# A graph layer on one core: PE's pipeline goes from three chunks to five, and the index loads get another release

## The reference

```python
h = jnp.maximum(_layernorm(x, axis=-1), 0.0)
e_feat = jnp.concatenate([h[src], h[dst], edge_attr], axis=-1)   # 412500 x 96
v = jax.nn.relu(e_feat @ W1 + b1) @ W2 + b2                      # 96 -> 64 -> 32
x_cand = jax.ops.segment_max(v, dst, num_segments=12500)
out = x + jnp.maximum(x_cand, h)
```

## Time and profile before

| what | value |
|---|---|
| median of three runs | 5345.29 us (5330.25 to 5361.33) |
| the profiled execution | 5326.15 us |
| its span | 5324.3 us |
| PE busy | 3680.6 us, 69% |
| PE weight load busy | 2578.9 us, 48% |
| GpSimd busy | 2701.2 us, 51% |
| VectorE busy | 2212.2 us, 42% |
| ScalarE busy | 982.3 us, 18% |
| mean granted TensorE clock | 0.829 |

### The profile page before, as it was taken

The page is one execution under the profiler, slowest core; times in us unless marked ns, Lnnn a source line. Parts: engine busy times, 40 slices in busy tenths (PEclk is TensorE's granted clock), DMA queues, the critical chain, the costliest instruction groups (busy, mean ns, idle before and its releaser), DMA issues.

```text
span 5324.3 us, 74917 instructions
## 1 busy us (share of the span) xinstructions
PE 3680.6 (69%) x19060; PEld 2578.9 (48%) x19060; DVE 2212.2 (42%) x6394; ACT 982.3 (18%) x2055; POOL 2701.2 (51%) x2853
## 2 busy tenths in 40 slices
PE   1577676667766777767776667676766767667777
PEld 1355454444544454545555445454544544445545
DVE  4344334344433444434444334343443443334436
ACT  2111111111111111111111111111111111111111
POOL 5455555554545455555555454555555555545551
PEclk9788888788888888888888888887887888878889
DMA  4222222222222222222222212222222222212222
GB/s 112 56 45 43 41 43 41 41 41 44 44 41 41 42 45 43 43 41 46 44 43 44 41 38 44 41 45 40 43 42 40 43 45 43 41 40 46 43 42 39
DMA packets 612176, 237.39 MB, mean 45 GB/s; under 512 B 328651, under 2 KB 609632, under 8 KB 612158
## 3 DMA queue, kind: packets, MB, share of 16 engines
q1 hardware_dynamic: 411534, 137.78, 10.7%
q0 software_dynamic: 91008, 46.57, 9.0%
q10 hardware_dynamic: 109616, 52.85, 3.4%
HBM read 227.75 MB, written 9.11 MB: 44 GB/s over the span
## 4 chain that ended last, share of the span: by engine, by line
another core or an unknown queue 43%; PE 29%; issue 14%; DVE 6%; ACT 5%; DVEq 1%; ACTq 1%; DMA 1%; SPq 0%
PE ps_spare L593 9%; PE ps_hid L547 5%; PE ps_hid L537 5%; PE ps_hid L543 3%; DVE hot L931 2%; PE ps_val L556 2%; PE ps_picked L578 2%; ACT hidden L726 2%; PE ps_turned L567 2%; PE ps_feat L528 2%; ACT feat_t L736 1%; ACT ps_biased L747 1%; DVE best L980 1%; ACTq L683 1%
## 5 line engine op out<-in xcount | busy, mean ns | idle before, releaser
L473 POOL DMA_INDIRECT feat<-h_rows,idx_ring x2824 | 2690.0, 953 | 2528.5 <-DMA idx_ring<-src_in 1661.4
L593 PE MATMUL ps_spare<-hot,table 128*128 128x256 f32 x10028 | 1920.8, 331 | 223.8 <-issue 221.0
L593 PEld LDWEIGHTS ps_spare<-hot,table 128*128 128x128 f32 x10028 | 1508.2, 212 | 574.4 <-issue 539.7
L980 DVE TENSOR_TENSOR best<-ps_picked,best 32x64 f32 x1612 | 354.8, 220 | 1495.6 <-remote 1358.8
L537 PE MATMUL ps_hid<-feat_t,w_blk 128*128 128x512 f32 x806 | 554.3, 777 | 515.9 <-ACT feat_t L736 387.0
L931 DVE TENSOR_SCALAR hot<-key_ring,class_at 128x256 fp32r<-128x256 f16 x2613 | 787.4, 369 | 98.3 <-remote 67.3
L726 ACT ACTIVATE hidden<-ps_hid,b_col 128x512 f32<-128x512 f32 x403 | 277.3, 688 | 1954.3 <-remote 1081.2
L567 PE MATMUL ps_turned<-ident,running 128*128 128x128 f32 x806 | 180.7, 310 | 567.9 <-DVE running L945 345.4
L547 PE MATMUL ps_hid<-edge_hot,term_ring 128*128 128x512 f32 x806 | 555.1, 776 | 0.7 <-DVE edge_hot L953 0.7
L967 DVE TENSOR_TENSOR ends<-ps_turned,ends 128x256 fp32r<-128x256 f32 x403 | 170.4, 423 | 731.7 <-ACT ends L731 416.3
L938 DVE SCALAR_TENSOR_TENSOR masked<-key_ring,group_at,ps_spare 128x256 f32<-128x256 f16 x400 | 174.0, 477 | 652.5 <-remote 584.3
(11 more groups left out here) (112 smaller groups left out, 1467.5 us busy)
## 6 DMA issues: line engine op xcount, KB each, us to landing
attr_ring<-edge_attr_in ACTq DMA_DIRECT2D x403, 128.0 KB
loc_ring<-loc_rows SPq DMA_DIRECT2D x403, 128.0 KB
feat<-h_rows,idx_ring POOLq DMA_INDIRECT x2824
keep_ring<-keep_rows SPq DMA_DIRECT2D x403, 64.0 KB
key_ring<-key_rows SPq DMA_DIRECT2D x201, 128.0 KB
term_ring<-term_rows SPq DMA_DIRECT2D x806, 16.0 KB
idx_ring<-src_in SPq DMA_DIRECT2D x403, 4.0 KB
end_ring<-end_rows SPq DMA_DIRECT2D x403, 2.0 KB
```

Of the source, the lines that this page charges most:

```text
L473: nc.gpsimd.indirect_dma_start(feat[:, slot, k, 0:D], None, h_dram, bass.IndirectOffsetOnAxis(ap=idx_ring[:, slot, k:k + 1].bitcast(U32), ...
L593: mm = pe.matmul(row_sums[t], table[half][:, at:at + Q, :].rearrange("p t d -> p (t d)"), hot[:, c, :], start=(c == 0 and t == 0 and half ...
L980: mm = nc.vector.tensor_tensor(col, ps_pick[D * q:D * q + D, WIN * q:WIN * q + WIN], col, ALU.max)
```

## The change

It does the following.

- PE's step now has features of v, first layer of v-1, second layer of v-2, turned ends of v-3 and picks of v-4. The selects of a batch lie in the last three gaps of an odd step and the first four of the next one. The steps of ScalarE and VectorE follow.
- PRE, the number of steps written out ahead of the loop, goes from 3 to 11; FULL = 3 takes over its other meaning, the chunks whose eight columns are all gathered.
- SyncE loads the index columns of chunk s when the gathers of chunk s-8 have landed. GpSimd then waits for `feat_turned` of chunk s-8 before it overwrites the slot. LAG goes from 2 to 4.
- `masked` gets two buffers by parity of the batch; the key rows are released by the mask of four batches before.
- The memset of `best` is split: the part that the start does not use is cleared early, the rest before the loop.

```diff
-PRE = 3
-LAG = 2
+FULL = 3
+PRE = 11
+LAG = 4
@@ SyncE
-            def step(s, slot, at):
-                sp.wait_ge(S["feat_turned"], s - (RING - 1))
+            def step(s, slot, turn, at):
+                sp.wait_ge(s_gather[slot], got(slot, turn - 1))
+                sp.sem_inc(S["idx_begun"], 1)
                 load_idx(at, slot)
                 if not known(s) or s - LAG >= RING:
                     sp.wait_ge(S["pick_ready"], s - (LAG + RING - 1))
                 load_aux(s - LAG, (slot - LAG) % RING)
@@
-                sp.wait_ge(S["mask_done"], i * 8 + 2 * (n - KEYS + 2))
+                sp.wait_ge(S["mask_done"], i * 8 + 2 * (n - KEYS + 1))
@@ GpSimd
                 pool.wait_ge(s_idx[slot], (i + v // RING) * 16 + 16)
+                if not known(i) or v >= RING:
+                    pool.wait_ge(S["feat_turned"], i * RING + (v - RING + 1))
@@ PE: first_layer
-                    pe.wait_ge(S["mask_done"], m * 2 + 4)
+                    pe.wait_ge(S["mask_done"], m * 2 + 2)
@@ PE: select
-                    if c == 0:
-                        pe.wait_ge(S["mask_done"], m * 2 + 2)
+                    if c == 0 and not (known(m) and m == 0):
+                        pe.wait_ge(S["mask_done"], m * 2)
@@ PE: order of a step
-            GAPS = (((0, 1), (2,), (3, 4), (5,), (6,)), ((7, 8), (9, 10), (11, 12), (), ()))
+            GAPS = (((6, 7), (8, 9), (10, 11), (12,), ()), ((), (), (0, 1), (2, 3), (4, 5)))
             def step(i, v):
...
+                m = i * 4 + (v - 1) // 2
+                gaps = GAPS[v % 2] if v else ((),) * 5
+                turn_features(i, v)
+                select(m, gaps[0])
+                if v >= 1:
+                    first_layer(i, v - 1)
                 select(m, gaps[1])
+                if v >= 2:
+                    second_layer(i, v - 2)
                 select(m, gaps[2])
+                if v >= 3:
+                    turn_ends(i, v - 3)
                 select(m, gaps[3])
+                if v >= 4:
+                    pick_ends(i, v - 4)
                 select(m, gaps[4])
@@ ScalarE
             def step(i, v, at):
+                take_features(i, v, at)
                 if later(i, v):
                     rectify(i, v - 1)
                 if later(i, v - 1):
+                    add_bias(i, v - 2)
+                if later(i, v - 2):
+                    take_ends(i, v - 3)
@@ VectorE
+            EARLY, LATE = range(0, 6), range(6, CLASSES)
             def step(i, v):
+                place_edges(i, v)
+                if v % 2 == 0:
+                    build_hot(i, v // 2, EARLY)
+                else:
+                    build_hot(i, v // 2, LATE)
+                if v >= 2:
                     scan(i, v - 2)
+                if v >= 2 and v % 2 == 0:
+                    mask_rows(i, v // 2 - 1)
+                if v >= 3:
+                    split_ends(i, v - 3)
+                    place_ends(i, v - 3)
+                if v >= 4:
+                    keep_best(i, v - 4)
```

More of the change, by code:

```diff
@@ L60, in gnn_layer @@
     assert ONE_TILE
-    assert D == 32 and HID == 64 and W2.shape[1] == D and (C - PRE) % RING == 0
+    assert D == 32 and HID == 64 and W2.shape[1] == D and (C - PRE) % RING == 0 and (C - FULL) % 2 == 0
     FULLP = N // T
@@ L152, in gnn_layer @@
         key_part = [z.bitcast(I32).rearrange("p (b e) -> p b e", b=NB)
-                    for z in (any_dst_h[:].rearrange("p b c -> p (b c)"), masked[:].rearrange("p t e -> p (t e)"))]
+                    for z in (any_dst_h[:].rearrange("p b c -> p (b c)"), masked[:, 0, :, :].rearrange("p t e -> p (t e)"))]
         key_stage = key_ring[:].rearrange("p k c a e -> p (k c a e)")[:, 0:NB * 2 * MIX].rearrange(
@@ L240, in got @@
             per = 16 * (COLS - 1)
-            return 16 * COLS + turn * per if slot < PRE else turn * per + per
+            return 16 * COLS + turn * per if slot < FULL else turn * per + per
         def any_steps(eng, any_step):
@@ L404, in _ @@
             for s in range(RING, ahead):
-                step(s, s % RING, s * CE)
+                step(s, s % RING, s // RING, s * CE)
             with sp.Fori(0, turns) as i:
@@ L412, in _ @@
             for s in range(ahead + RING * turns, C):
-                step(s, s % RING, s * CE if s < C - 1 else LAST)
+                step(s, s % RING, s // RING, s * CE if s < C - 1 else LAST)
                 if s % 2 == 0:
@@ L419, in _ @@
             next_key(0, BATCHES)
+            next_key(0, BATCHES + 1)
             sp.wait_ge(S["feat_turned"], C)
@@ L537, in first_layer @@
                 pe.matmul(ps_hid[:], w1_blk[:], feat_t[:, two, :], start=True, stop=False, skip_group_check=True)
-                if not known(i) or v >= PRE:
-                    m, part = i * 4 + (v - PRE) // 2, (v - PRE) % 2
-                    pe.wait_ge(S["mask_done"], m * 2 + 4)
+                if v >= FULL:
+                    m, part = i * 4 + (v - FULL) // 2, (v - FULL) % 2
+                    pe.wait_ge(S["mask_done"], m * 2 + 2)
                     for t in range(2):
-                        pe.matmul(ps_hid[HID:P, 2 * P:3 * P], w1_rep[:], masked[:, t, MIX * part:MIX * part + MIX],
+                        pe.matmul(ps_hid[HID:P, 2 * P:3 * P], w1_rep[:], masked[:, (v - FULL) // 2 % 2, t, MIX * part:MIX * part + MIX],
                                   start=False, stop=False, skip_group_check=True)
@@ L635, in clear_mixed @@
                 pe.wait_ge(S["cols_cleared"], RING)
-            steps(pe, step, {1: begin_mixed, PRE - 1: clear_mixed})
+            steps(pe, step, {0: begin_mixed, RING - 1: clear_mixed})
             first_layer(0, C - 1)
+            second_layer(0, C - 2)
+            turn_ends(0, C - 3)
+            pick_ends(0, C - 4)
+            second_layer(0, C - 1)
             turn_ends(0, C - 2)
-            second_layer(0, C - 1)
+            pick_ends(0, C - 3)
+            turn_ends(0, C - 1)
             pick_ends(0, C - 2)
-            turn_ends(0, C - 1)
             pick_ends(0, C - 1)
@@ L837, in _ @@
             nc.vector.memset(h_win[:, T - 1:Q * TG, :], 0.0).then_inc(S["pads"], 1)
-            for slot in range(PRE, RING):
+            for slot in range(FULL, RING):
                 nc.vector.memset(feat[:, slot, Q - 1, 0:D], 0.0).then_inc(S["cols_cleared"], 1)
@@ L905, in _ @@
             nc.vector.tensor_copy(key_stage[:, :, 1, :], high).then_inc(S["key_staged"], 1)
-            for t in range(2):
-                nc.vector.memset(masked[:, t, :], 0.0).then_inc(S["mask_done"], 1)
             dve.wait_ge(S["const_ready"], 5)
@@ L918, in _ @@
             nc.vector.engine_nop().then_inc(S["const_ready"], 1)
+            dve.wait_ge(S["loc_staged"], NB)
+            nc.vector.memset(best[:, T * HID:NP_ROWS], 0.0).then_inc(S["best_zero"], 1)
             node_terms(dve, nc.vector.tensor_copy, 1)
@@ L938, in mask_rows @@
                     nc.vector.scalar_tensor_tensor(
-                        out=masked[:, t, :].rearrange("p (c e) -> p c e", c=2), in0=key_ring[:, n % KEYS, :, 1, :],
+                        out=masked[:, n % 2, t, :].rearrange("p (c e) -> p c e", c=2), in0=key_ring[:, n % KEYS, :, 1, :],
                         scalar=group_at[:, t:t + 1], in1=row_sums[t].rearrange("p (c e) -> p c e", c=2),
@@ L1019, in _ @@
             dve.wait_ge(S["firsts_in"], 32)
-            steps(dve, step, {1: check})
+            dve.wait_ge(S["term_stored"], 16 * (1 + len(h_parts)))
+            nc.vector.memset(best[:, 0:T * HID], 0.0).then_inc(S["best_zero"], 1)
+            steps(dve, step, {0: check})
             scan(0, C - 2)
+            split_ends(0, C - 3)
+            place_ends(0, C - 3)
+            keep_best(0, C - 4)
+            scan(0, C - 1)
+            split_ends(0, C - 2)
+            place_ends(0, C - 2)
+            keep_best(0, C - 3)
+            split_ends(0, C - 1)
             place_ends(0, C - 1)
-            split_ends(0, C - 2)
             keep_best(0, C - 2)
-            scan(0, C - 1)
-            split_ends(0, C - 1)
             keep_best(0, C - 1)
```

67 lines of the change are left out of this document (14 added, 53 removed).

## The result

The changed kernel takes **5474.51 us** (median of four runs, 5470.36 to 5485.17). The kernel before, run beside it, takes 5337.77 (5261.16 to 5361.33). The ratio is 1.0341 with a 95% interval of 1.0223 to 1.0459: slower, where I forecast 4985 us and faster. The ratio counts fast runs only, for the kernel before the two of 5330.25 and 5261.16 us, which is why it is above the 1.0256 of the two medians. The profiled execution took 5477.52 us.

The account below looks back on a forecast made before the run. PE's semaphores, late while gathers fly, were taken to bound the loop. Lull 7.2, three chunks at 8.73 and landing 2.7 gave 11.9 us per chunk; 403 x 11.9 plus 189 gave 4985 us, range 4820 to 5260 (8 in 10: 4450 to 5520).

Parts of the forecast that it names:

- What bounds the kernel: The loop: while gathers are in flight PE works on, but its semaphores reach other engines late, over 4 us in one chunk.
- (a): PE's new step order: answers wanted a full step later, worth from nothing to 5.1 us per chunk.
- (c) and (d): Helper and key loads trailing further and two masked buffers, 0; split memset and deeper fill and drain, +10 us taken.
- short link: Class 0 of a batch waits for the previous batch's masking, an estimated 4.5 us; may stop PE once in two chunks.
- (b): Index load and GpSimd's wait: load released by landed gathers but queued behind helper loads; -2.60 to +4.6 us per chunk.
- lull: Time from PE's burst of signals until GpSimd starts gathering: 7.2 us after the change instead of 2.60.
- The sum: Cycle of lull 7.2, n chunks of gathers at 8.73 and landing 2.7 us, giving the period and 4985 us.
- n=3: Gathers in runs of three chunks (n is chunks per run), 11.9 us per chunk; n=2 would give 13.5.
- 19 us free: PE's unhindered time per three-chunk cycle: 7.7 step of tolerance, 7.2 lull, 4.5 of prompt signals, against 23 us needed.
- GpSimd starts later and its runs pair up: Rival at SyncE's queue: index load behind helper loads, runs of two chunks, 13.5 us per chunk, 5630 us; chance 0.30.
- Full gain: Rival: index load hidden nearly always, PE hardly ever stopped; 10.05 us per chunk, 4240 us; chance 0.16.
- The skill's trap: Rival: VectorE's fast modes lock GpSimd out of writing descriptors; gathers at an assumed 1.1 us, 5410 us; chance 0.03.

Follow-up runs that it names:

- late_gate: after_idx_ahead with GpSimd's chunk s also waiting until SyncE has issued the helper rows of s-5: 5284.68 us, 0.9874 of the kernel before.
- after_idx_ahead: The changed kernel with SyncE loading the index columns of s+2 in step s, ahead of its waits on PE: 4743.66 us, 0.8865 of the kernel before.
- grp_3_4: after_idx_ahead with each chunk's seven gathers in groups of three and four, GpSimd waiting between groups for their landing: 6131.4 us, 1.1506 of the kernel before.

## Why the prediction was wrong

**What bounds the kernel.** Right: the gathers make PE's signals late, and that is the loop (3151 us without them). One half of my sentence was wrong, "PE works on, but its semaphores reach the others late". In a long run PE itself stops, with no answer missing: "issue" ahead of single selects. From 2000 to 4000 us it is 84 us in the kernel before and 274 in the one after, at L593 and L598:

```profile
L593 PE MATMUL ps_spare<-hot,table 128*128 128x256 f32 x3900 | 753.5, 333 | 85.2 <-issue 84.0 <-DVE hot L931 0.9
...
L598 PE MATMUL ps_spare<-hot,table 128*128 128x256 f32 x3762 | 751.1, 342 | 439.5 <-issue 273.7 <-DVE masked L947 157.3 <-DVE best L989 7.7
```

Nor is it PE alone: SyncE's issues spread in a run too (2.9 us between two helper loads above). At the start 59 gathers run in a row, not the 56 that I counted, since three of the eight chunks gather eight columns; nothing hangs on it.

**(a) PE's order.** I gave nothing to 5.1 us a chunk. Measured, with (c) and (d) in it: 241 us with the old release (5351 to 5111 in its group), 94 with the load ahead, so 0.2 to 0.6 us. The short link that I named is there: the 157 us of waiting for `masked` above.

**(b) The index load.** The mechanism was right and the lull a little long. Between two runs I had 2.7 us of landing and burst and 7.2 of lull, 9.9 together; the trace has 9.1 on average, 8.05 to 9.82 in the four rows above. In the cycle shown, 3.2 us pass to the burst (3012.93 to 3016.12) and 5.3 from there to the first gather (3021.42). Its sign I left open, -2.60 to +4.6 us per chunk; it is a loss of 0.9 (5111 to 5475), and late_gate shows the lateness by itself, 541 us or 1.3 per chunk.

**(c) and (d).** Taken as neutral and +10 us. PE's wait at the start went from 17.25 to 12.77 us. No run did these parts alone, so their worth stays open.

**The sum: the step that failed.** "I take n=3, 11.9 us." The cycle has n=2, in 72 of 74 runs. The formula was nearly right: it gives 27.1 us for a cycle of two and the trace has 26.6 on average, 25.9 to 27.0 in the rows above; 403 chunks at 13.2 us are what the kernel takes. What failed is the reach of PE, "19 us free". I added PE's step of tolerance, the lull, and 4 to 5 us of prompt signals as if PE ran on at its own speed in a run. It went from one turn of features to the next in 18.4 us, three matmuls in some 7 us of it, so a third pick came in time in one of 74 runs. The row for it stood in front of me: picks recorded until 3072.26 with no answer before 3082.03, in a run of just two chunks. A tolerance of one step of 7.7 us can't span 10 us in which the engine that should use it is stopped as well.

**The rivals.** "GpSimd starts later and its runs pair up" is what happened, with the place and n as written. 13.5 us and 5630 were 2 to 3% too high (13.2 by the rows, 5475), since 9.1 us and not 9.9 lie between two runs. Its sign was there too, a period above 13 us with "remote" waits near 15 (12.8). I gave it 0.30 because PE's tolerance "is doubled or more", which counted steps and not time. "Full gain" does not come by this change, but after_idx_ahead shows how near it was: 11.3 us, still with late signals (7.66 us "remote" above, 1412 us in the whole run), not 10.05. "The skill's trap", from the Trainium skill, "SBUF — State Buffer", "Who interferes with whom": the trace agrees with it in kind, at a price far below the 1.1 us a gather that I assumed. From 2000 to 4000 us, 61 of the 219 gathers that run beside VectorE's `hot` or `edge_hot` take longer than 0.96 us, up to 1.19 (the one at 3008.17 above takes 1.01); of the 832 others none does, though many run beside other VectorE work. On average that is less than 10 ns a gather, and the mean stays at 949 to 958 ns in every kernel that gathers seven columns. By "TensorE: Matmul & The Clock Gate", "The cost: per-tile semaphore tail" (Trainium skill), a signal costs 26 ns; that may hold where nothing is gathered, but 12.8 us ahead of a copy is not in it.

## What to carry to other kernels

A load's release is not only the semaphore that its wait names but all that its queue has ahead of it: count the waits and issues between, and put the load whose landing starts a long stretch of work first, a chunk or two ahead. When a resource runs in bursts that silence another, a later start of the burst makes it longer, and the loss feeds itself; take the cycle's length from the time that the slower party really gets, not from how many steps it may run ahead. And test a reordering with each of its halves alone: here one half was worth 4.5%, the other cost 7%, and done differently it gave 7% more.

## What the runs showed of the hardware

- PE's signals come 4 to 15 us late while GpSimd's indirect gathers are in flight (3008.97 to 3013.19, 3000.86 to 3016.12 above), and PE and SyncE issue more slowly. Little is being moved: 43 GB/s by all of the core's transfers together, and the gathers' queue has a fifth of the bytes (46.57 of 237.59 MB). Plain transfers from the same queue don't do it (3112 us), nor do indirect ones in runs of at most four (3168 and the groups of grp_3_4). What in the chip does it stays open.
- It isn't there always. One group of runs had none of it (3640 us for the kernel before, 5326 to 5351 in the others), with gathers just as long. It ran on a chip of the same number as the last group, in which the kernel before took 5326. So whether it belongs to a chip or to a chip's condition at the time stays open. What these kernels gain against each other holds only where the delay is.
- An indirect gather of 128 rows takes GpSimd 0.95 us and 0.30 to the next; a plain one 0.55. In grp_3_4 it has landed 2.2 us after its record where nothing else moves, and 3.9 to 5.2 after it where, in the case read, the chunk's loads of 128 KB are under way. VectorE's `hot` and `edge_hot` can lengthen the record of a gather beside them, from 0.95 to at most 1.2 us.
- PE's clock is given back with the delay: 0.80 in the changed kernel, 0.87 with the load ahead, 0.99 without gathers. A pair of wide matmuls takes 2.08 us behind a stop and 1.02 in a free stretch, so part of each gain is the clock's; it was not separated.
- Not tried: a limit on how far PE may run ahead, and a looser pace of the gathers without waits for a landing. No complete version tried beats after_idx_ahead (4718 to 4744 us, 11.4 to 11.6% below the kernel before).
